# Other places in the scan for the shared expert's pieces and for seven small steps around them, and its output added onto x by VectorE straight from the bank

## The reference

```python
x = x + conv(layernorm_over_channels(x))      # pixel shuffle, a Mamba block over 2304 positions, unshuffle
#   the Mamba block: h = exp(dt*A)*h + (dt*u)*B at each position, 256 channels x 16 states; y = sum_n h*C
t = layernorm(tokens(x))
y = sum over 2 of 8 experts: (silu(t @ w1[e]) * (t @ w3[e])) @ w2[e] * weight
shared = (silu(t @ sw1) * (t @ sw3)) @ sw2    # one expert that sees every token, 512 -> 1024 -> 512
x = tokens(x) + y + shared
```

## Time and profile before

| | |
|---|---|
| median of the two runs | 2513.24 us (2512.12 and 2514.36) |
| the profiled execution's own time | 2514.68 us |
| its span, first to last instruction | 2512.9 us |
| busy: TensorE, VectorE, ScalarE, GpSimd | 2163.7, 1300.5, 1031.0, 1220.7 us |
| the scan of image 0 (6 chunks) | to 372.4 us |
| the scan of images 1 to 3 (18 chunks, six groups) | 372.4 to 1366.3 us |
| the rest: last two groups, routing, 43 expert tiles, output | to 2512.9 us |

### The profile page before, as it was taken

The page is one execution under the profiler, slowest core; times in us unless marked ns, Lnnn a source line. Parts: engine busy times, 40 slices in busy tenths (PEclk is TensorE's granted clock), DMA queues, the critical chain, the costliest instruction groups (busy, mean ns, idle before and its releaser), DMA issues.

```text
span 2512.9 us, 30004 instructions
## 1 busy us (share of the span) xinstructions
PE 2163.7 (86%) x8124; PEld 1181.8 (47%) x8125; DVE 1300.5 (52%) x2051; ACT 1031.0 (41%) x2087; POOL 1220.7 (49%) x1133
## 2 busy tenths in 40 slices
PE   4577778888888888888877878999999999999995
PEld 3233435555555545555544653444444444444443
DVE  2499998887987888879887401111111111111112
ACT  2678777666666776766763110111111011111010
POOL 1598997787877777878865161111111111111110
PEclk7676788988988989989988999999999999999997
DMA  3555555444555454445552541131313223131116
GB/s 122 138 153 151 142 149 134 118 116 125 131 133 132 126 131 125 116 120 133 137 133 87 200 156 28 25 125 18 124 25 125 84 67 117 24 125 25 25 21 159
DMA packets 158600, 271.83 MB, mean 108 GB/s; under 512 B 18496, under 2 KB 105640, under 8 KB 155904
## 3 DMA queue, kind: packets, MB, share of 16 engines
q1 hardware_dynamic: 147264, 247.65, 34.8%
q0 software_dynamic: 11200, 22.63, 5.0%
HBM read 222.63 MB, written 51.79 MB: 109 GB/s over the span
## 4 chain that ended last, share of the span: by engine, by line
PE 55%; DVE 16%; issue 12%; ACT 6%; DMA 5%; POOL 4%; SPq 1%; DVEq 0%; POOLq 0%; ACTq 0%
PE pair L1773 20%; PE single L1785 12%; DVE WALL L1234 11%; PE pair L1533 5%; PE single L1451 3%; DMA u<-xrows,gix 3%; PE pair L1539 2%; PE single L1446 2%; POOL slots L718 2%; DVE pair L1215 2%; PE pair L1624 2%; ACT WALL L951 1%; POOL WALL L683 1%; PE single L1519 1%; PE single L1473 1%
## 5 line engine op out<-in xcount | busy, mean ns | idle before, releaser
L683 POOL TENSOR_TENSOR WALL<-WALL 128x768 f32<-128x768 f32 x384 | 695.4, 1815 | 179.6 <-DVE WALL L1234 124.8
L1234 DVE TENSOR_TENSOR_SCAN WALL<-WALL,carry,pair 128x384 f32<-128x384 f32 x640 | 611.2, 996 | 0.2
L1773 PE MATMUL pair<-WALL,zz 128*128 x1376 | 599.3, 593 | 1.8 <-ACT zz L1049 1.0
L951 ACT ACTIVATE WALL<-WALL,AnR 128x384 f32<-128x384 f32 x768 | 420.0, 607 | 77.7 <-DVE WALL L1234 67.4
L1773 PEld LDWEIGHTS pair<-WALL,zz 128*128 128x128 f32 x1376 | 258.7, 191 | 311.8 <-issue 311.8
L751 POOL DMA_INDIRECT yrows<-sp,aix x43 | 68.2, 1586 | 689.9 <-ACT sp L1061 637.6
L1363 DVE SCALAR_TENSOR_TENSOR sp<-XA,tab,pair 128x512 f32<-128x512 f32 x86 | 64.3, 747 | 591.6 <-ACT XA L1055 591.6
L1533 PE MATMUL pair<-XA,WALL 128*128 128x288 f32 x1024 | 306.2, 452 | 9.7 <-DVE XA L1171 9.7
L1785 PE MATMUL single<-WALL,sp 128*128 x688 | 303.1, 593 | 2.7 <-issue 1.5
L1055 ACT ACTIVATE XA<-pair 128x512 f32<-128x512 f32 x86 | 51.4, 597 | 578.8 <-PE pair L1773 578.8
L1533 PEld LDWEIGHTS pair<-XA,WALL 128*128 128x128 f32 x1024 | 214.9, 214 | 89.2 <-issue 19.8
(11 more groups left out here) (247 smaller groups left out, 2364.7 us busy)
## 6 DMA issues: line engine op xcount, KB each, us to landing
WALL<-dtd SPq DMA_DIRECT2D x384, 192.0 KB, 3.9
WALL<-in_L_ffn_w_dram SPq DMA_DIRECT2D x24, 2048.0 KB, 13.7
WALL<-wsd SPq DMA_DIRECT2D x144, 256.0 KB, 2.9
WALL<-crows SPq DMA_DIRECT2D x96, 192.0 KB, 3.8
dtd<-sp SPq DMA_DIRECT2D x96, 192.0 KB, 3.1
WALL<-wsd SPq DMA_DIRECT2D x16, 768.0 KB, 4.8
X<-in_x_dram SPq DMA_DIRECT2D x4, 1152.0 KB, 6.7
xrows<-rows SPq DMA_DIRECT2D x24, 192.0 KB, 2.1
```

The source lines that it names most:

```text
L683: pool.tensor_tensor(hC[m], hs[:, (NS * j + n) % HRING, :, :], Cs[k][:, n % NPH // 2, :].unsqueeze(1).to_broadcast([P, HALF, T]), ALU.mult ...
L951: a = nsc.activation(dA[(NS * j + n) % AHEAD][:, e, :], dtR[:, h * NQ + c + e, :], ACT.Exp, scale=AnR[:, c + e, h, q:q + 1])
L1234: scan = nv.tensor_tensor_scan(hs[:, m, e, :], dA[(NS * j + n) % AHEAD][:, e, :], dBu[e], init, ALU.mult, ALU.add)
L1773: last = mm(bank[2 * w + q][:, :], xT[k][:, r, :], WALL[:, ds(off + (w * RR * I + r * I + q * 512), 512)], start=(r == 0), stop=(r == RR - 1))
```

## The change

Five tables give the steps. Of the three rows of `PIECE_AT` the second is the old order; a negative step is one of the chunk before (-4 is its step 12), and `H1_OUT` counts on into the next chunk.

```diff
+        PIECE_AT = ((-4, -2, 0, 2, 4, 6, 8, 10), (-2, 0, 2, 4, 6, 8, 10, 12), (-2, -1, 2, 3, 6, 7, 9, 10))
...
+        H1_OUT = (3, 5, 7, 9, 11, 13, 15, 17)
...
+        Y_OUT = (1, 5, 9, 12)
...
@@ ScalarE
-                            if phase == 2 and n in (6, 10, 14):
-                                y_to_x(G, b - 1, j // GC, (n - 6) // 4, E1)
...
-                        if late3 and n == 8:
-                            rows_copy(g - 3, 1 - k, M1)
...
+                        if late3 and n == 7:
+                            rows_copy(g - 3, 1 - k, M1)
                         if front and n == 7:
                             abs_relu(g + 1, 0)
                             exps(g + 1)
...
-                        if n == 12:
+                        if n == 11:
                             if behind:
                                 out_copy(g - 1, bb, bj)
...
@@ VectorE
-                        if not first and j % GC == 2 and n == 14:
-                            v.wait_ge(e_ps, 3 * PH * group_of(b, j) + 3 * PH)
-                            nv.tensor_copy(xgroup(b - 1, j // GC, RR - 1), E1).then_inc(e_y, 1)
+                        if not first and j % GC == 2 and n in Y_OUT:
+                            r = Y_OUT.index(n)
+                            v.wait_ge(e_ps, 3 * PH * group_of(b, j) + 2 * PH + 2 * r + 2)
+                            xv = xgroup(b - 1, j // GC, r)
+                            nv.tensor_tensor(xv, xv, E1, ALU.add).then_inc(e_y, 1)
...
@@ TensorE, down_piece: without b no identity product
-                if part2 == 1:
+                if part2 == 1 and b is not None:
                     last = mm(ps, ident[:, :], xgroup(b, half, r), start=False, stop=True)
...
@@ TensorE, the step
-                        if n == 6:
+                        if n == 4 and front0:
+                            pe.wait_ge(f_abs, 2 * g + 4)
+                            mean_of(xchunk(b if j < JC - 3 else b + 1, (j + 3) % JC), f_mean, M0[:, STAT:STAT + CP])
+                        if n == 5 and behind:
                             after(pe, f_abs, 2 * g + 4 if front else 2 * NCH)
-                            if front0:
-                                mean_of(xchunk(b if j < JC - 3 else b + 1, (j + 3) % JC), f_mean, M0[:, STAT:STAT + CP])
-                            if behind:
-                                out_product(g - 1, bb, bj)
-                        if front1 and n in (9, 10):
-                            u_first(g + 2, k, n - 9)
-                        if front1 and n in (11, 12):
-                            u_second(g + 2, k, n - 11)
+                            out_product(g - 1, bb, bj)
+                        if front1 and n in (8, 9):
+                            u_first(g + 2, k, n - 8)
+                        if front1 and n in (10, 12):
+                            u_second(g + 2, k, (n - 10) // 2)
```

More of the change, by code:

```diff
@@ L450, in batch, with weights @@
                     front = not (last and j == JC - 1)
-                    def weights(q):
-                        if not first and not (last and j == JC - 1 and q + WRING >= PH):
-                            next_piece(b, j, q)
+                    def weights(at):
+                        for q in range(PH):
+                            if FETCH_AT[j % GC][q] == at and not first and not (last and j == JC - 1 and q + WRING >= PH):
+                                next_piece(b, j, q)
                     if front:
@@ L474, in batch @@
                         spread_dtu(g + 1, 1 - k, 0)
+                    weights(6)
+                    if front:
                         spread_dt(g + 1, 1 - k, 1)
@@ L962, in batch @@
                             G, phase = group_of(b, j), j % GC
-                            if phase == 0 and n >= 4 and n % 2 == 0:
-                                h1_copy(G, n // 2 - 2, E1)
-                            if phase == 1 and n in (0, 2):
-                                h1_copy(G, n // 2 + 6, E1)
-                            if phase == 2 and n in (6, 10, 14):
-                                y_to_x(G, b - 1, j // GC, (n - 6) // 4, E1)
+                            for q in range(PH):
+                                if phase == H1_OUT[q] // NS and n == H1_OUT[q] % NS:
+                                    h1_copy(G, q, E1)
                         if n == 2:
@@ L1222, in batch @@
                             gate_y(g, k, 0)
-                        if not first and j % GC == 1 and n % 2 == 0:
-                            shared_gate(group_of(b, j), n // 2, E1)
-                        if not first and j % GC == 2 and n == 14:
-                            v.wait_ge(e_ps, 3 * PH * group_of(b, j) + 3 * PH)
-                            nv.tensor_copy(xgroup(b - 1, j // GC, RR - 1), E1).then_inc(e_y, 1)
+                        if not first and j % GC == 1 and n in GATED_AT:
+                            shared_gate(group_of(b, j), GATED_AT.index(n), E1)
+                        if not first and j % GC == 2 and n in Y_OUT:
[3 more added lines that the diff above has]
+                            nv.tensor_tensor(xv, xv, E1, ALU.add).then_inc(e_y, 1)
                         v.wait_ge(m_dA, i + 1)
@@ L1534, in up_piece, with down_piece @@
                 last.then_inc(e_ps, 1)
-            def down_piece(w, b, half, q, ps):
+            def down_piece(w, half, q, ps, b=None):
                 r, part2 = q // 2, q % 2
                 for kk in range(RR):
-                    last = mm(ps, w[:, kk, :], act8[:, part2 * RR + kk, :], start=(part2 == 0 and kk == 0), stop=False)
-                if part2 == 1:
+                    last = mm(ps, w[:, kk, :], act8[:, part2 * RR + kk, :], start=(part2 == 0 and kk == 0),
+                              stop=(b is None and part2 == 1 and kk == RR - 1))
+                if part2 == 1 and b is not None:
                     last = mm(ps, ident[:, :], xgroup(b, half, r), start=False, stop=True)
@@ L1563, in piece @@
                         pe.wait_ge(e_y, RR * G + q // 2)
-                    down_piece(w, b, half, q, E1)
+                    down_piece(w, half, q, E1)
             def piece_last(G, ph, q):
@@ L1704, in batch @@
                             projections(g + 2, k)
-                        if not first and n % 2 == 0 and n < 14:
-                            piece(group_of(b, j), b - 1, j // GC, j % GC, n // 2 + 1)
-                        if n == 14 and not (last if j == JC - 1 else first):
-                            if j == JC - 1:
-                                piece(group_of(b + 1, 0), b, 0, 0, 0)
-                            else:
-                                piece(group_of(b, j + 1), b - 1, (j + 1) // GC, (j + 1) % GC, 0)
+                        for q in range(PH):
+                            if not first and PIECE_AT[j % GC][q] == n:
+                                piece(group_of(b, j), b - 1, j // GC, j % GC, q)
@@ L1712, in _ @@
+                        for q in range(PH):
+                            if PIECE_AT[(j + 1) % GC][q] == n - NS:
+                                if j == JC - 1 and not last:
+                                    piece(group_of(b + 1, 0), b, 0, 0, q)
+                                elif j < JC - 1 and not first:
+                                    piece(group_of(b, j + 1), b - 1, (j + 1) // GC, (j + 1) % GC, q)
             batches(pe, batch)
```

6 lines of the change are left out of this document (4 added, 2 removed).

## The result

The changed kernel takes 2425.28 us (median of 2424.27 and 2426.30); the ratio to the kernel before is 0.965, 95% interval 0.9609 to 0.9692. The prediction's sum was 2429.4. The profiled execution took 2424.27 us with a span of 2422.5, so 90.4 us less than the profiled execution of before; by the medians it is 88.0.

A forecast was written before the change was run, and what follows sets the result against it. VectorE bounds the scan, its 147.5 us of waits mostly due to late TensorE; 55.5 stay and additions cost 8.1, so 83.9 are won: 2514.7 - 83.9 - 1.4 = 2429.4 us, range 2392 to 2468.

The forecast's parts named there:

- The size: Six groups of the shared expert: of VectorE's 147.5 us of waiting, 55.5 stay; 83.9 us won after the additions' cost.
- The additions: VectorE, six groups: four additions instead of one copy, 18 more instructions of 0.452 us, cost 8.1 us.
- `rows_copy`: ScalarE, all thirds: moved ahead of the softplus, it lets gate_logits start at about 553 against 558.0.
- moves that I cost at nothing: Mean and out_product two and one steps sooner, ScalarE's copies of both in step 11, SP's places: no cost counted.
- Start of the second third: Piece 7 made in step 10, not 12, brings ScalarE's block 4.2 us sooner; waits 13.46 become 2.7 us (1.2 to 5).
- First third: TensorE idles 3.6 us before piece 4 and restarts slow; 4 us of waits stay a group (1.4 to 6).
- Last third: Identity products and the wait for output 3's copy go; 2.5 us stay (0.5 to 5), for a pair's second piece.
- The clean pipeline: Rival, whole scan: all lower bounds hold, 20.8 us of waits stay, 118.6 won, 2395; chance 22%.
- TensorE stays the late one: Rival: the copy behind the softplus holds TensorE as rows_copy did; 91.5 us stay, 47.9 won, 2464; chance 15%.
- The half clock: Rival: short waits keep TensorE's clock at 0.72, a group takes 181 us against 166, 2603 in all; chance 4%.
- No scan waited for GpSimd: Scans waiting for GpSimd was listed as a sign that the forecast is wrong; no size given.

The follow-up runs named there:

- e1: Kernel before with only rows_copy moved from ScalarE's step 8 to step 7, ahead of the softplus: 2467.4 us, ratio 0.9814.
- e5: Changed kernel with the first third's pieces, their copies and SP's places for them back in the old steps: 2424.7 us, ratio 0.9652.
- e11: Changed kernel with only the convolution's taps back in TensorE's steps 9 to 12: 2417.3 us, ratio 0.9615.
- e7: Changed kernel with ScalarE's copy of the first third's piece 3 made inside the softplus, not behind it: 2408.8 us, ratio 0.9583.
- e3: Changed kernel with the old identity products and copies of the shared expert's outputs in place of VectorE's additions: 2426.4 us, ratio 0.9648.
- e9: Changed kernel with piece 3's copy inside the softplus, residue in step 2, second third's piece 1 before dt_product, second addition in step 6: 2391.9 us.
- e4: Changed kernel with rows_copy back in ScalarE's step 8, behind the softplus: 2481.8 us, ratio 0.987.
- e6: Changed kernel with mean and out_product back in TensorE's step 6, taps in 9 to 12, ScalarE's copies in 12: 2457.9 us, ratio 0.9772.

## Why the prediction was right, and where its reasons were not

**The size.** 147.5 - 55.5 = 92 us of waits were to go, 93.1 went. The additions were to cost 8.1 us; by the rows they do, 10.8 against the 2.7 of the copies of before. VectorE's busy time rose by only 3.6. Rows overlap by some 0.1 us when one follows the other without a wait (549.51 starts before 549.04 + 0.56 in the stretch shown above), so that fewer waits make less busy time: the groups by line sum to 927.4 us before and 934.1 after, 6.7 more, and exceed the busy time by 81.0 and 84.1. So 3.1 of the 4.5 us are overlap, and the other 1.4 are rows that got shorter. The two differences, 1.1 and 4.5, make the 5.6 by which 89.5 beats the forecast 83.9.

**`rows_copy`: right.** `gate_logits` starts with its products in every third, and the move is worth 46.5 us alone and 56.5 in the new order. A miss of detail: "the softplus itself comes 0.58 us later" left out that ScalarE may now wait for the transposes first, as in e1 (second third of group 1):

```profile
437.29 0.59 ACT L870 ACTIVATE rows<-single 96x512 f32<-96x512 f32 x1 [1.50 <-PE single L1512]
```

Behind it the residue waits 0.6 us in two chunks of image 0 in which VectorE did not wait before.

**The step that failed: "moves that I cost at nothing".** Mean, `out_product` and ScalarE's copies of both were costed at nothing, for their inputs are there in time. Together they are worth 40.6 us. The sentence "in the second third nothing else is in the way, in the last third neither" holds only because of them: without them `z_first` waits 2.97 us for the mean copy, also behind the softplus, and all that is queued behind it on TensorE comes later. The forecast got the sum right since it assumed that nothing else was in the way and the change, for another reason, saw to it: that is luck. The same question that found `rows_copy` (who else waits for a step of ScalarE behind the softplus?) would have found this.

**Start of the second third: right by its rows, wrong about the gain.** 2.7 us a group were left, 13.7/6 = 2.3 stay; the residue keeps 1.3 to 1.6 where 1.2 was forecast. That the new places of the first third's pieces do this is shown by e5, whose second thirds wait 15.1 us more. But the first third pays 19.7 for it. So of the 85 to 90 us of the change these places bring nothing; `rows_copy`, mean and `out_product` without anything else give 93.

**First third: right in mechanism, not in its parts.** 4 us were left, 32.0/6 = 5.3 stay, or 4.9 without the loop's turn (2.9). TensorE was to idle 3.6 us before piece 4 and restart slow: 4.29, and 3.75 us for the piece. The spread for step 8 was to come 2 us sooner; it comes 0.8 later against the chunk's start (549.04 - 523.7 = 25.3, before 564.90 - 540.4 = 24.5). The copy of the piece was put where the old trace had ScalarE; the prediction says that ScalarE "comes 1 to 2 us later" without the stalls, and did not put that into this term. The copy that the piece of step 4 waits for comes 21 us after the chunk's start (544.65 - 523.7); the one of step 8 came 16.6 us after it before, and by the prediction's 560.1 the piece would have started 19.7 after it, where it starts 21.4 after it. The gating grew to 2.07, of which e11 shows 1.29 to be the taps, near the 1.5 forecast. e7 shows nearly the whole cause to be the copy's place: 5.5 us are left there, 3.0 of them at the loop's turn.

**Last third: right.** 2.5 a group for the first five, 8.7/5 = 1.7 measured, all of it additions waiting for a piece, 2.0 at the longest. That the additions and not copies do this is worth nothing by e3; that was not forecast, since the sum took the copy's wait off without a price for what would have replaced it.

**The rivals.** The clean pipeline (2395) did not come: the first third alone is some 20 us off it. e9, with four more edits, comes 3 us below it. "TensorE stays the late one" (2464; its terms give 2514.7 - 47.9 - 1.4 = 2465) is near what e4 and e6 show, 2482 and 2458, each with a part of the change undone. The half clock did not take over: 0.90 to 0.95 in the groups. No scan waited for GpSimd.

**The Trainium skill's rule** ("TensorE: Matmul & The Clock Gate", "Why this matters for your kernels") was weighed for the last third: the loss of the full rate lies with long idle gaps, so that short waits would cost nothing. The traces do not agree that a short wait is always free. In the changed kernel the same piece of two groups comes behind the same instructions and the same 2.01 us without work:

```profile
524.30 3.87 PE L1541 MATMUL pair<-XA,WALL 128*128 128x288 f32 x8 [2.01 <-ACT XA L888]
...
676.04 2.18 PE L1541 MATMUL pair<-XA,WALL 128*128 128x288 f32 x8 [2.01 <-ACT XA L888]
```

The granted clock is 0.56 over the first and 1.00 over the second. So a slow piece behind a short gap can come, as the prediction took it to, but need not.

## What to carry to other kernels

A wait that ends with a late copy can be the first of several consumers behind one long stretch of another engine (here `rows_copy`, the mean copy and the copy of a piece behind the softplus): list all that wait for what stands behind the stretch, for the next one can take the place of the one that is removed. A move that costs nothing can still carry the gain, as filler of an engine's time before a wait that stays. And when the bounding engine no longer waits, the next late engine shows, so that what one third wins can come back in part in the next (9.7 of 26.5 us here, with GpSimd late): measure by stages, and in pairs.

## What the runs showed of the hardware that was not expected

The same gap on TensorE can be followed by either clock. In e1_rows_early the windows from `z_first` to the end of `out_product`'s first part (columns as in the earlier trace rows), after the same 2.97 us without work:

```profile
449.09:455.69 6.60, 6.60 (x18) 4.74 (x19) 3.93 (x7) 2.38 (x6) 6.42 (x6) 0.55 0.59 150
606.42:610.16 3.74, 3.74 (x18) 2.90 (x19) 3.74 (x7) 2.38 (x6) 3.56 (x4) 1.00 0.45 142
```

The granted clock is 0.55 of 2.4 GHz in the one, nearly all at 1.2 GHz, and 1.00 in the other; the same 18 passes take 6.60 us and 3.74. The gate behind them waits 4.82 and 1.94. So a gap's price is two prices in one execution, 2.9 us apart here, and a sum from one trace takes the one that it happens to show.
